# Products of exponentials and values issued alternately into the array's two column halves

## The reference, cut to what matters

```python
def _L1_attn_ref(x, query_proj, key_proj, value_proj, output_proj):
    KEY_DIM = 16
    q = jnp.einsum('bnd,hkd->bnhk', x, query_proj)
    k = jnp.einsum('bnd,hkd->bnhk', x, key_proj)
    v = jnp.einsum('bnd,hvd->bnhv', x, value_proj)
    sim = jnp.einsum('bnkh,bmhk->bnhm', q, k)
    scale = jnp.asarray(1.0 / np.sqrt(KEY_DIM), dtype=sim.dtype)
    attn = jax.nn.softmax(sim * scale, axis=1)
    o = jnp.einsum('bnhm,bmhv->bnhv', attn, v)
    return jnp.einsum('bnhv,dhv->bnd', o, output_proj)
```

## Time and profile before

| | us |
|---|---|
| median of three timed runs | 4378.24 (4377.39 to 4380.41) |
| the profiled execution, first to last instruction | 4382.6 |
| PE busy in it | 3673.3 |
| DVE busy | 2821.0 |
| ACT busy | 2427.6 |
| POOL busy | 999.9 |

### The profile page before, as it was taken

One profiled execution on the slowest core, in us unless ns is written; L12 is line 12 of the kernel. 1 busy time (PEld: TensorE's weight loads), 2 busy tenths in 40 slices (PEclk: granted clock), 3 DMA queues, 4 the chain that ended last, 5 costly groups with the idle time before them and its releaser, 6 DMA issues.

```text
span 4382.6 us, 66677 instructions
## 1 busy us (share of the span) xinstructions
PE 3673.3 (84%) x19970; PEld 1761.1 (40%) x20144; DVE 2821.0 (64%) x4828; ACT 2427.6 (55%) x5081; POOL 999.9 (23%) x719
## 2 busy tenths in 40 slices
PE   4678798898988889898888889898888989898876
PEld 3445343444443344444344444444434444343321
DVE  3562676667676766767676676767667676767432
ACT  2343565565656566565656656565655656565432
POOL 1210222112222221222222221223221122222110
PEclk7689899999999999999999999999999999999987
DMA  2002001010000101010010101000010100001010
GB/s 60 1 3 75 8 18 43 18 47 15 32 27 15 46 16 45 19 43 12 15 46 19 43 18 44 18 23 32 18 43 18 47 15 30 29 12 46 15 49 13
DMA packets 112589, 124.19 MB, mean 28 GB/s; under 512 B 12434, under 2 KB 85692, under 8 KB 112188
## 3 DMA queue, kind: packets, MB, share of 16 engines
q1 hardware_dynamic: 112124, 119.26, 8.4%
q0 software_dynamic: 64, 0.01, 0.0%
HBM read 64.70 MB, written 54.53 MB: 27 GB/s over the span
## 4 chain that ended last, share of the span: by engine, by line
PE 50%; issue 22%; DVE 17%; ACT 5%; POOL 5%; DVEq 1%; SPq 1%; DMA 0%; POOLq 0%; ACTq 0%
PE pb L569 23%; PE o_bank L569 14%; PE s L569 4%; PE pb L695 3%; PE y_bank L569 2%; PE pb L664 2%; DVE nmax L1284 2%; POOL scratch L1369 2%; POOL scratch L1364 2%; DVE stat L1178 1%; POOL vsc L1402 1%; DVE stat L1199 1%; DVE scratch L1191 1%; ACT ex L1016 1%; PE pb L719 1%
## 5 line engine op out<-in xcount | busy, mean ns | idle before, releaser
L1284 DVE TENSOR_REDUCE nmax<-s 128x1 f32<-128x512 f32 x1024 | 687.3, 683 | 693.2 <-PE s L569 689.7
L569 PE MATMUL o_bank<-ex,vsc 128*64 128x512 f32 x2048 | 1008.9, 639 | 34.9 <-POOL vsc L1402 33.0
L1016 ACT ACTIVATE ex<-s,nmax 128x512 f32<-128x512 f32 x1024 | 697.7, 685 | 556.0 <-DVE nmax L1284 508.7
L1402 POOL TENSOR_TENSOR vsc<-vrow,rinv 128x256 f32<-128x256 f32 x256 | 189.5, 740 | 1964.2 <-DVE rinv L1292 1961.6
L569 PEld LDWEIGHTS o_bank<-ex,vsc 128*64 128x64 f32 x2048 | 279.0, 147 | 666.2 <-issue 594.1
L1364 POOL TENSOR_TENSOR scratch<-scratch 128x1024 f32<-128x1024 f32 x128 | 314.0, 2453 | 776.9 <-DVE scratch L1191 641.5
L569 PE MATMUL s<-qs,ks 96*128 96x512 bf16 x1024 | 365.7, 392 | 102.8 <-ACT ex L1016 92.7
L569 PE MATMUL pb<-wqkv,hsh 128*128 128x512 f32 x768 | 390.0, 644 | 47.0 <-DVE hsh L1171 41.8
L569 PE MATMUL pb<-kT,qT 64*64 64x64 f32 (+1 forms) x6144 | 325.7, 254 | 37.3 <-issue 16.4
L664 PE MATMUL pb<-const,scratch 128*128 128x128 f32 x1024 | 184.9, 340 | 198.7 <-POOL scratch L1369 196.8
L1369 POOL TENSOR_TENSOR scratch<-scratch,stat 128x1024 f32<-128x1024 f32 x128 | 255.8, 1999 | 266.5 <-DVE stat L1203 266.1
(11 more groups left out here) (193 smaller groups left out, 6190.7 us busy)
## 6 DMA issues: line engine op xcount, KB each, us to landing
parts_store<-side SPq DMA_DIRECT2D x64, 384.0 KB, 2.6
qs<-parts_store SPq DMA_DIRECT2D x128, 192.0 KB, 2.7
ks<-parts_store SPq DMA_DIRECT2D x128, 192.0 KB, 3.1
parts_store<-side SPq DMA_DIRECT2D x64, 256.0 KB, 2.8
parts_store<-side SPq DMA_DIRECT2D x64, 128.0 KB, 2.7
xin<-in_L_attn_x SPq DMA_DIRECT2D x16, 256.0 KB, 4.2
ex<-in_L_ffn_w SPq DMA_DIRECT2D x16, 256.0 KB, 3.1
out<-yrow SPq DMA_DIRECT2D x16, 256.0 KB, 3.6
```

What stands on the lines that cost most here:

```text
L569: return pe.matmul(o, l, r, start=start, stop=stop, skip_group_check=True)
L1016: A(ex[:, h % 2, m, :], s_bank[c % 2][:], ACT.Exp, bias=nmax[:, c % 8:c % 8 + 1], accum_out=rsum[:, h % 2, m:m + 1]).then_inc(GA, 1)
L1284: V.tensor_reduce(nmax[:, c % 8:c % 8 + 1], s_bank[c % 2][:], X, ALU.max, negate=True).then_inc(GV, 1)
L1402: G.tensor_tensor(vsc[:, h % 2], vrow[:, :, V1 * h:V1 * h + V1], rinv[:, h % 2, :].unsqueeze(2).broadcast_to([P, 4, V1]), ALU.mult).then_i ...
```

## The change

A step `av` no longer has four key tiles of one head, but two key tiles of both heads of a pair. Steps of `sim`, `scale_v` and `av` are counted by w, 0 to 15, in place of the head h. The pair is w // 2; the even w has its key tiles 0 and 1, the odd w its tiles 2 and 3. Within a step j runs from 0 to 3: the head's parity is j % 2 and the key tile 2 (w % 2) + j // 2. So the products of `av` go into partitions 0 to 63, 64 to 127, 0 to 63, 64 to 127, and both halves of the bank are summed over an even and the following odd step: the first two products of the even step start the sums, the last two of the odd step end them. `scale_v` takes from `vrow` the two heads' values of two key tiles, in one instruction as before. A few waits stand in another order before the same instruction. The written-out orders of all four engines are new; in that of PE 167 of 235 steps stand at another place, by at most 12. Sizes, counts and buffers are the same.

```diff
 def glob_steps():
     s = []
-    for h in range(H1 + 1):
-        for m in range(4):
-            if h < H1:
-                s += [("sim", h, m)]
-            if h and m == 0:
-                s += [("scale_v", h - 1)]
-            if h and m == 1:
-                s += [("av", h - 1)]
-            if h and h % 2 == 0:
-                p = h // 2 - 1
-                s += {2: [("o", p)], 3: [("proj", p)]}.get(m, [])
+    for w in range(H1 + 1):
+        for j in range(4):
+            if w < H1:
+                s += [("sim", w, j)]
+            if w and j == 0:
+                s += [("scale_v", w - 1)]
+            if w and j == 1:
+                s += [("av", w - 1)]
+            if w and w % 2 == 0:
+                p = w // 2 - 1
+                s += {2: [("o", p)], 3: [("proj", p)]}.get(j, [])
...
@@ -786,28 +786,29 @@
                     mm(s_bank[n % 2][:], xn1[:, P * (n // 2):P * (n // 2) + P], wv1[:, 512 * (n % 2):512 * (n % 2) + 512])\
                         .then_inc(GE, 1)
                 elif kind == "sim":
-                    _, h, m = s
-                    c = 4 * h + m
-                    g = h // G1
-                    if m == 0 and h % G1 == 0:
+                    _, w, j = s
+                    c = 4 * w + j
+                    g = w // 2
+                    par, m = j % 2, 2 * (w % 2) + j // 2
+                    if j == 0 and w % 2 == 0:
 
                         pe.wait_ge(stack_loaded[g % 2], (b * (GROUPS // 2) + g // 2 + 1) * STACK_COUNT)
                     if c >= 2:
                         need(pe, glob, "act", b, ("sim", (c - 2) // 4, (c - 2) % 4), "e")
                     else:
                         need(pe, glob, "act", b, ("values", 2 * NT - 2 + c), "v")
-                    mm(s_bank[c % 2][:], ks[:, g % 2, h % G1, P * m:P * m + P], qs[:, g % 2, h % G1, :]).then_inc(GE, 1)
+                    mm(s_bank[c % 2][:], ks[:, g % 2, par, P * m:P * m + P], qs[:, g % 2, par, :]).then_inc(GE, 1)
                 elif kind == "av":
-                    h = s[1]
-                    need(pe, glob, "pool", b, ("scale_v", h), "v")
-                    if h % 2 == 0:
-                        if h:
-                            need(pe, glob, "act", b, ("o", h // 2 - 1), "t")
+                    w = s[1]
+                    if w % 2 == 0:
+                        if w:
+                            need(pe, glob, "act", b, ("o", w // 2 - 1), "t")
                         else:
                             need(pe, glob, "act", b - 1, ("o", 7), "t")
-                    for m in range(4):
-                        last = mm(o_bank[V1 * (h % 2):V1 * (h % 2) + V1, :], vsc[:, h % 2, m, :], ex[:, h % 2, m, :],
-                                  start=(m == 0), stop=(m == 3))
+                    need(pe, glob, "pool", b, ("scale_v", w), "v")
+                    for j in range(4):
+                        last = mm(o_bank[V1 * (j % 2):V1 * (j % 2) + V1, :], vsc[:, w % 2, j, :], ex[:, w % 2, j, :],
+                                  start=(w % 2 == 0 and j < 2), stop=(w % 2 == 1 and j >= 2))
                     last.then_inc(GE, 1)
...
@@ -1005,16 +1006,16 @@
                 elif kind == "sim":
-                    _, h, m = s
-                    c = 4 * h + m
+                    _, w, j = s
+                    c = 4 * w + j
+                    if j == 0:
+                        if w >= 2:
+                            need(act, glob, "pe", b, ("av", w - 2), "o")
+                        else:
+                            need(act, glob, "pe", b - 1, ("av", H1 - 2 + w), "o")
                     need(act, glob, "dve", b, s, "max")
-                    if m == 0:
-                        if h >= 2:
-                            need(act, glob, "pe", b, ("av", h - 2), "o")
-                        else:
-                            need(act, glob, "pe", b - 1, ("av", H1 - 2 + h), "o")
-                    A(ex[:, h % 2, m, :], s_bank[c % 2][:], ACT.Exp, bias=nmax[:, c % 8:c % 8 + 1],
-                      accum_out=rsum[:, h % 2, m:m + 1]).then_inc(GA, 1)
+                    A(ex[:, w % 2, j, :], s_bank[c % 2][:], ACT.Exp, bias=nmax[:, c % 8:c % 8 + 1],
+                      accum_out=rsum[:, w % 2, j:j + 1]).then_inc(GA, 1)
...
@@ -1278,18 +1279,18 @@
-                    _, h, m = s
-                    c = 4 * h + m
+                    _, w, j = s
+                    c = 4 * w + j
                     need(dve, glob, "pe", b, s, "s")
                     V.tensor_reduce(nmax[:, c % 8:c % 8 + 1], s_bank[c % 2][:], X, ALU.max, negate=True).then_inc(GV, 1)
                 elif kind == "scale_v":
-                    h = s[1]
-                    need(dve, glob, "act", b, ("sim", h, 3), "e")
-                    if h >= 2:
-                        need(dve, glob, "pool", b, ("scale_v", h - 2), "v")
-                    else:
-                        need(dve, glob, "pool", b - 1, ("scale_v", H1 - 2 + h), "v")
-                    V.reciprocal(rinv[:, h % 2, :], rsum[:, h % 2, :]).then_inc(GV, 1)
+                    w = s[1]
+                    if w >= 2:
+                        need(dve, glob, "pool", b, ("scale_v", w - 2), "v")
+                    else:
+                        need(dve, glob, "pool", b - 1, ("scale_v", H1 - 2 + w), "v")
+                    need(dve, glob, "act", b, ("sim", w, 3), "e")
+                    V.reciprocal(rinv[:, w % 2, :], rsum[:, w % 2, :]).then_inc(GV, 1)
...
@@ -1391,16 +1392,19 @@
                 if s[0] == "scale_v":
-                    h = s[1]
+                    w = s[1]
+                    p, m = w // 2, 2 * (w % 2)
+                    if w == 0:
+                        need(pool, glob, "act", b, ("values", 2 * NT - 1), "v")
+                    if w >= 2:
+                        need(pool, glob, "pe", b, ("av", w - 2), "o")
+                    else:
+                        need(pool, glob, "pe", b - 1, ("av", H1 - 2 + w), "o")
                     need(pool, glob, "dve", b, s, "r")
-                    if h == 0:
-                        need(pool, glob, "act", b, ("values", 2 * NT - 1), "v")
-                    if h >= 2:
-                        need(pool, glob, "pe", b, ("av", h - 2), "o")
-                    else:
-                        need(pool, glob, "pe", b - 1, ("av", H1 - 2 + h), "o")
-                    G.tensor_tensor(vsc[:, h % 2], vrow[:, :, V1 * h:V1 * h + V1],
-                                    rinv[:, h % 2, :].unsqueeze(2).broadcast_to([P, 4, V1]), ALU.mult).then_inc(GP, 1)
+                    G.tensor_tensor(vsc[:, w % 2].rearrange("p (m a) d -> p m a d", a=2),
+                                    vrow[:, m:m + 2, 2 * V1 * p:2 * V1 * (p + 1)].rearrange("p m (a d) -> p m a d", a=2),
+                                    rinv[:, w % 2, :].rearrange("p (m a) -> p m a", a=2).unsqueeze(3).broadcast_to([P, 2, 2, V1]),
+                                    ALU.mult).then_inc(GP, 1)
```

More of the change, by code:

```diff
@@ L243 @@
 ORDER = {
[L244 to L250, removed]
+    "pe": ("2ga3g2a2gsaga2gagsg3ag2a2g2agsagasgag2s2a2gsas2gsg3a2g3ag2a3g3a2gagsagags3g3a3g2agsa2gas4agags3as4ag"
+           "a2ga6ga2g2a2g2aga2gags6a2g2sg5a2gs5a6g2a2g4agas2ag4agasag2a2g2ag5a2gag4ags2ags2gagsa2gsaga3ga"),
+    "act": ("ga4gag4as2gags2asa2g5a2gs3agsag2s3a4g3asg2a2gsag3a2g2a2gsgag2s5g2as2a2sags2g2asasa2s2a3gaga5ga2g2a2g"
+            "a2gag4ag5a2g2a2g3asg2ags3as2g2ag7a2ga2g4a2gs2as2agsag2agsgasga2gsg2sa4g"),
+    "dve": ("a5gsa2gas2g2aga3g2asgsa3g3as2gsasa3g2sa2gs2agsa3g2a2gs3ga2gasa3gs2asgsasgasgagasa2s2as5a6g5a2gs3a2ga"
+            "sgags2asg2a3gsa2gasg2a2sa2gs2agag2a2sgag2asg2agsgas2a2ga3gasga2gag2s2ga"),
+    "pool": ("2g3ag2ag3a2g2s6g2ag2asagas2agsgs2g"),
 }
```

## The result

The kernel after takes 3999.56 us (median of four runs, 3996.54 to 4002.86) against 4379.32 us for the kernel before (four runs this time, 4377.39 to 4384.98): a ratio of 0.9126, 95% interval 0.9113 to 0.9139, 380 us less. The forecast was 4010 us.

The account below looks back on a forecast made before the run. PE, fullest engine at 84% busy, was taken as the bound, `o_bank` products its largest group. 14 periods x (24 - 1.7) = 312 us, plus 45 and 12, made 369; 4382.6 - 369 - 4.4 = 4009, said as 4010 us, range 3890 to 4135.

Parts of the forecast that it names:

- Step (1): In a step `av`, both halves stream at once: four slots, not eight, 3.64 to about 1.92 us at full clock.
- Rivals B: Products of `av` start in strict program order, so three slots are won, not four: 4101 us; chance 10%.
- E: In `av`, the two halves' streams don't overlap at 512 columns, so nothing moves: 4378 us; chance 3%.
- F: In `av`, each change of half first empties the array, making the kernel slower: 4504 us; chance 3%.
- Step (2): Of 29.1 us freed on PE per period, 24 us (82%) shortens the period; at least 20 us (68%).
- if the rewritten orders fill every hole: Upper bound on the period's gain: all 29.1 us freed on PE reach the period.
- Step (3): PE's granted clock falls from 0.95 to 0.94 in a period, costing 2.0 us, 1.7 of it on the path.
- Rival D: The clock falls to 0.87, costing 176 us more in 14 periods: 4186 us; chance 8%.
- Step (4): GpSimd's scaling `vsc` in its new walk stays at 0.61 us, cost 0; at worst 44 us in all.
- Step (5): Waits of `av`, `sim` and `scale_v` and SP's loads stay the same in another order: cost 0.
- Step (6): Outside full periods: 45 us gained in the drain from 4131 us on, about 12 us in ten other steps.
- Rival C: Lane `a` holds the period at 242 us, so the gain is 205 us: 4173 us; chance 10%.

Follow-up runs that it names:

- Experiment 3: The kernel after, but a step issues its four products to half 0, 0, 1, 1 in place of 0, 1, 0, 1: 4003.19 us, ratio 0.9138.
- Experiment 1: The kernel after (new steps), but with the four written-out orders of the kernel before: 4152.55 us, ratio 0.9480.
- Experiment 6: New steps with the orders of before, a step's last product pair issued twice (six slots) or left out (two slots): 4248.54 and 4098.01 us.

## Why the prediction was right, point by point

**Step (1), the slots.** Right. 1.94 us against 1.92. The pairs of the earlier trace rows hold for 512 columns as for 65, with 0.01 us on top for a pair. The whole group is busy for 547 us, 27 over the 520 that I gave. Half clock has a part in it: the mean clock is 0.73 from 3760 us to the end, against 0.80 in the last stretch of before. Rivals B, E and F are out. Experiment 3 adds what the earlier trace rows could only suggest, that starts aren't in program order. The rule of the Trainium skill (TensorE: Matmul & The Clock Gate, The mechanism) is strict order. For products into two column halves the starts in these traces go against it: 0.013 us in place of four slots in experiment 3.

**Step (2), the share.** The number was right (24 us forecast before the clock, 23.2 measured with it), its lower bound wrong. I took 68 to 73% as the least, from the share of `o_bank` in the chain and from the pass of lane `a` without `glob`. Experiment 1 has the orders of before, for which both readings were made, and passes 49%. Experiment 6 has the share fall from 56% over 41% to 23%: even the first pair of slots passes less than was read. What made up for it is the term that I had only as "if the rewritten orders fill every hole": 150 us, for which I had no row. So that 82% came out is in part luck. Had the change left the orders alone, the time would have been 4153 us, 143 over the forecast and outside its range. (VectorE's share, given as 77%, is 76% by its own numbers; measured, 74%.)

**Step (3), the clock.** Forecast 0.94, measured 0.94, but its cost was smaller than the 2.0 us that I had: the time at half clock rose by 3.2 us a period, PE's busy time within it fell by 0.8, and all products other than `o_bank` together are busy for 0.7 us longer. Rival D was a small one here, but it is the largest thing behind the bend: with two slots the clock is 0.90.

**Step (4), GpSimd.** `vsc` stays at 0.61 us (median 612 ns in both). Right.

**Step (5), waits.** Nearly right. By the groups of eleven periods the `o_bank` products waited for `vsc` for 4.2 us before and 28.6 after, 0.4 and 2.6 us a period, since PE now comes sooner. I had that at nothing.

**Step (6), fill and drain.** From the last `hsh` copy to the end it is 463.2 us against 528.8, 65.6 less. A period (22.3) and 45 for the drain make 67. Up to the third `hsh` copy it is 564.4 against 579.5, 15 less, where I had 12. The 13 periods between give 307 us, where 13 x 22.3 is 290. The sum is 388 us of span, forecast 369.

**Rival C.** Out: its floor of 242 us for a period was too high. But a hold of this kind is near. With two slots the period is 226.5 us, against 214 if PE's time in `o_bank` alone counted.

## What to carry to other kernels

Products with 64 output partitions use half the array's columns: give both halves work within one step, with at most four instructions of one half in a row (here four cost nothing and eight cost four slots), and the pair costs what one does. When a change takes time from a full engine whose order is written out by hand, lay out the orders anew and price the two together: here the products alone passed 49% of their gain and with new orders 81%, and either part without the other misleads. A chain's share overstates what a large cut returns: here it was 73%, and 56, 41 and 23% passed. Before cutting further, lengthen and shorten the step by the same amount and see whether the slope is the same on both sides.

## What was not expected of the hardware

A product passed three waiting instructions of the other column half and started 0.013 us after the first; with eight in front it waited for four slots. Useless products in a wait of 6 to 7 us made the kernel 14 to 22 us faster, as the time at half clock fell from 29.4 to 21 or 22 us a period. And two useful products less in each step returned only 35 of 235 us, of which the slower clock kept more than the waits. A VectorE multiplication of 16 elements for each of 128 partitions, 0.17 us by itself, took up to 1.95 us when it started beside certain GpSimd instructions, and then ended just after them.
